# The first attention's convolutions by pairs with its weight work spread out, and unread matmuls in four stage tails and ahead of the third attention

## The reference

```
q, k, v = x @ Wq.T, x @ Wk.T, x @ Wv.T
q = silu(causal_group_conv(q, Wq_conv) + bq)   # 4 taps, one group of 128 channels per head
k = silu(causal_group_conv(k, Wk_conv) + bk)
gate, beta = sigmoid(x @ Wg.T + bg), sigmoid(x @ Wb.T + bb)
St = beta_t * St + k_t v_t^T                   # per head, over the 256 tokens of a sequence
out_t = (q_t . St) * gate_t
out = out @ Wo.T
```

## Time and profile before

| | us |
|---|---|
| three timed runs | 3417.91, 3407.55, 3426.61 |
| their median | 3417.91 |
| profiled execution, its own time | 3410.35 |
| its span, first to last instruction | 3408.5 |
| busy: TensorE, VectorE, GpSimd, ScalarE | 2928.4, 2177.0, 1583.2, 1431.4 |
| mean granted TensorE clock | 0.924 |

### The profile page before, as it was taken

One profiled execution on the slowest core, in us unless ns is written; L12 is line 12 of the kernel. 1 busy time (PEld: TensorE's weight loads), 2 busy tenths in 40 slices (PEclk: granted clock), 3 DMA queues, 4 the chain that ended last, 5 costly groups with the idle time before them and its releaser, 6 DMA issues. The chain is left out here.

```text
span 3408.5 us, 59487 instructions
## 1 busy us (share of the span) xinstructions
PE 2928.4 (86%) x20634; PEld 2564.9 (75%) x20634; DVE 2177.0 (64%) x5538; ACT 1431.4 (42%) x3043; POOL 1583.2 (46%) x1530
## 2 busy tenths in 40 slices
PE   8979999999999899795698977649997858976798
PEld 6859989998898788694487866647775746966687
DVE  6756666666666667665735656548886655665755
ACT  3344555555455433343523333335554334433342
POOL 2333444434444414634605435548887456450743
PEclk9989999999999999897798987959998878988899
DMA  2022212121211200332102333510002352330333
GB/s 70 1 72 55 61 53 68 52 62 52 62 55 49 74 27 1 97 121 63 36 2 80 94 108 90 145 44 2 2 2 69 88 141 81 113 109 3 93 99 97
DMA packets 129129, 220.88 MB, mean 65 GB/s; under 512 B 18609, under 2 KB 68145, under 8 KB 128881
## 3 DMA queue, kind: packets, MB, share of 16 engines
q1 hardware_dynamic: 95026, 147.47, 14.5%
q0 software_dynamic: 21216, 57.96, 6.6%
q10 hardware_dynamic: 12672, 12.58, 1.1%
HBM read 170.23 MB, written 47.72 MB: 64 GB/s over the span
## 5 line engine op out<-in xcount | busy, mean ns | idle before, releaser
L1632 POOL DMA_INDIRECT MXG<-dxn,IDX x250 | 237.3, 949 | 231.6 <-PE bank L1204 167.6
L1642 POOL DMA_INDIRECT YG<-dyo,POSI x192 | 187.4, 976 | 210.6 <-DMA dyo<-YS 111.9
L2491 POOL TENSOR_SCALAR SX<-SX,MN 128x256 f32<-128x256 f32 x256 | 233.7, 928 | 56.4 <-DVE MN L2415 56.3
L1615 POOL TENSOR_TENSOR MWL<-RAW,MWH 128x608 fp32r<-128x608 f32 (+2 forms) x118 | 181.6, 1547 | 42.5 <-ACT MWH L1307 36.2
L1971 POOL TENSOR_TENSOR QL<-QG,QH 128x512 fp32r<-128x512 f32 x64 | 82.9, 1296 | 248.7 <-ACT QH L1826 248.7
L2415 DVE CUSTOM_DVE_ANT_0 SX<-bank,FMASK 128x128 f32<-128x128 f32 (+1 forms) x512 | 156.1, 351 | 50.7 <-PE bank L2305 50.5
L515 PE MATMUL bank<-MWH,GH 128*128 x500 | 172.3, 345 | 8.3 <-issue 4.5
L1026 POOL TENSOR_TENSOR HL<-HID,HH 128x512 fp32r<-128x512 f32 x56 | 72.4, 1293 | 224.2 <-ACT HH L993 223.7
L515 PE MATMUL bank<-MWH,SHH 128*128 128x256 f32 x352 | 111.5, 317 | 73.6 <-POOL SHL L1486 25.4
L1940 POOL TENSOR_TENSOR HWL<-RAW,HWH 128x640 fp32r<-128x640 f32 x68 | 113.3, 1676 | 120.3 <-DVE DEC L1857 120.0
L1329 ACT ACTIVATE GH<-bank 128x256 fp32r<-128x256 f32 x250 | 96.7, 387 | 171.7 <-PE bank L1204 166.0
(11 more groups left out here) (451 smaller groups left out, 11263.0 us busy)
## 6 DMA issues: line engine op xcount, KB each, us to landing
dyo<-YS SPq DMA_DIRECT2D x250, 128.0 KB
RAW<-in_wheads SPq DMA_DIRECT2D x68, 320.0 KB
RAW<-in_eL SPq DMA_DIRECT2D x64, 304.0 KB
BB<-dgates SPq DMA_DIRECT2D x68, 256.0 KB, 3.6
GB<-dgates SPq DMA_DIRECT2D x68, 256.0 KB, 4.3
dxn<-XN ACTq DMA_DIRECT2D x16, 512.0 KB
RAW<-in_eL SPq DMA_DIRECT2D x32, 256.0 KB
RAW<-in_sL SPq DMA_DIRECT2D x18, 384.0 KB
```

What stands on the lines that cost most here:

```text
L1615: nc.gpsimd.tensor_tensor(MWL[:, at_:at_ + cols], RAW[:, n % RAW_SLOTS, 0:cols], f32(MWH[:, at_:at_ + cols]), ALU.subtract).then_inc(w_rea ...
L1632: nc.gpsimd.indirect_dma_start(MXG[:, n % XGS, :], None, dxn, bass.IndirectOffsetOnAxis(ap=IDX[:, b:b + 1], axis=0)).then_inc(x_in[n % XGS ...
L1642: nc.gpsimd.indirect_dma_start(YG[:, i % YGS, :], None, dyo[0:m.blocks * P, :], bass.IndirectOffsetOnAxis(ap=POSI[:, c * NT + t:c * NT + t ...
L2491: nc.gpsimd.tensor_scalar(part, part, MN[:, n % RING2, 1:2], None, ALU.subtract).then_inc(s_less1, 1)
```

## The change

In the first attention:

- q gets the pair form of k; `EH`, `EL`, `EV`, `DF` exist once for q and once for k. Keys come first everywhere (`KEYS_FIRST`).
- TensorE's order in step s is now: projections of k, q; result of s-2; values of s; scores of s-1; convolutions of k, q.
- VectorE's order is: differences of k, q; add(s-2); low parts of the values; weigh(s-1); scans; low part of scores; `post` of k, q; QG.
- GpSimd no longer waits for `dec_done`; it makes `tap_sums` of both, each in the step of its weight piece (n = 0 and n = 1).
- SP's rows for n = 3 move behind the next head's weight loads.

In the tails of four sparse layers, ten unread matmuls after each tile's `x_done`, for slots k > `m.late`: 8 of 16 tiles after L1, 14 after L2. Ahead of attn2, 20 unread matmuls, and 6 in each of six slots.

```diff
-PAIR_COL = HEAD_COLS
-ALL_COLS = HEAD_COLS + 2 * P
+PAIR_COLS = (HEAD_COLS, HEAD_COLS + 2 * P)
+ALL_COLS = HEAD_COLS + 4 * P
+KEYS_FIRST = (1, 0)
...
+                for t in range(NT if nx and k > m.late else 0):
+                    if k == m.slot_of(t):
+                        pe.wait_ge(b_kept, st.blocks + m.blocks)
+                        pe.wait_ge(x_done, st.xd + t + 1)
+                        warm(10, 5 if nx.kind == 'moe' else 2)
...
-                    for q in range(2):
-                        if q and (s or not first):
-                            pe.wait_ge(post_done, done + s)
+                    for j, q in enumerate(KEYS_FIRST):
+                        if s or not first:
+                            pe.wait_ge(both_kept, done * 2 + (2 * s - 1 + j))
                         for k in range(KC):
                             last = mm3(bank[q][:, :], weights(hh, PRE_COLS[q][k]), xt(k, n * W, W), k == 0, k == KC - 1)
                         last.then_inc(pre_done, 1)
-                    if s or not first:
-                        scores(s - 1, done)
+                    if s >= 2 or not first:
+                        result(s - 2, done)
...
-                    pe.wait_ge(pre_ready, done * 2 + (2 * s + 1))
-                    for c in range(CK):
-                        last = mm3(bank[2][:, :].rearrange('p (b t) -> p b t', b=2), weights(hh, CONV_COLS[0] + c * P),
-                                   (QPH[:, :, c:c + S], QPL[:, :, c:c + S]), c == 0, c == CK - 1)
-                    last.then_inc(conv_done, 1)
...
+                    if s or not first:
+                        scores(s - 1, done)
...
+                    for j, q in enumerate(KEYS_FIRST):
+                        pe.wait_ge(pre_ready, done * 2 + (2 * s + j + 1))
                         for c in range(2):
...
+                            last = mm3(bank[q][:, 0:S].rearrange('p (b j) -> p b j', b=2), weights(hh, PAIR_COLS[q] + (1 - c) * P),
+                                       moved(q, EVEN, c), c == 0, c == 1)
+                        last.then_inc(conv_done, 1)
+                        pe.wait_ge(d_lo, done * 2 + (2 * s + j + 1))
+                        if s or not first:
+                            pe.wait_ge(post_done, done * 2 + (2 * s - 1 + j))
+                        for part in EDGE:
+                            for c in range(2):
+                                last = mm3(bank[2 + q][:, part * S:(part + 1) * S].rearrange('p (b j) -> p b j', b=2),
+                                           weights(hh, CONV_COLS[q] + EDGE_TAPS[part][c] * P), moved(q, part, c), c == 0, c == 1)
+                        last.then_inc(conv_done, 1)
...
+                    differences(s, 0, done)
+                    differences(s, 1, done)
+                    if s >= 2 or not first:
+                        add(s - 2, done)
+                    values_lo(s, 0, done)
+                    values_lo(s, 1, done).then_inc(v_ready, 1)
                     if s or not first:
                         weigh(s - 1, done)
+                        dve.wait_ge(p_done, done + s)
                     dve.wait_ge(rows_in[n], at(nc.vector, i, 64, 32 * (hh + 1) + 16))
+                    decay(n, 0)
+                    decay(n, 1).then_inc(dec_done, 1)
                     if s or not first:
                         scores_lo(s - 1, done)
...
+                    post(s, 0, done)
+                    post(s, 1, done)
+                    dve.wait_ge(silu_done, done * 2 + (2 * s + 2))
                     nc.vector.tensor_tensor(QG[:, :], QS[:, :], GB[:, n * W:(n + 1) * W], ALU.mult).then_inc(qg_done, 1)
...
-                    if PIECES_AT[n]:
-                        pool.wait_ge(dec_done, done + (s + 1))
-                    if n == 0:
-                        pool.wait_ge(raw_in[1], i * 32 + 16 * (rounds + hh + 2))
-                        tap_sums(1 - hh, i * 4 + 2 * (hh + 1))
...
                     for q in PIECES_AT[n]:
+                        if q < 2:
+                            pool.wait_ge(raw_in[q], i * 32 + 16 * (rounds + hh + 2))
+                            tap_sums(1 - hh, q, i * 8 + (4 * (hh + 1) + 2 * q))
                         piece_lo(1 - hh, q, done + (st.pieces + PIECES * (hh + 1) + q + 1))
...
-            pe.wait_ge(xt_lo, (st.tr + 1) * HALF)
             pe.wait_ge(w_ready, st.pieces + 4)
             pe.wait_ge(prepared, 14)
+            warm(20, 2)
+            pe.wait_ge(xt_lo, (st.tr + 1) * HALF)
             for s in SLOTS2:
+                if s < 0:
+                    warm(6, 2)
```

More of the change, by code:

```diff
@@ L308, in build @@
         GB = r.put('GB', [P, T])
[L309 to L313, removed]
+        EH = [r.put(n, [P, 3, 2, H2 + 1], F32R) for n in ('QEH', 'KEH')]
+        EL = [r.put(n, [P, 3, 2, H2 + 1], F32R) for n in ('QEL', 'KEL')]
+        EV = [r.put(n, [P, 2, H2]) for n in ('QEV', 'KEV')]
+        DF = [r.put(n, [P, 2, 2, H2]) for n in ('QDF', 'KDF')]
         QG = r.put('QG', [P, W])
@@ L1747, in pair @@
[L1747 to L1753, removed]
-                        for c in range(2):
-                            last = mm3(bank[3][:, part * S:(part + 1) * S].rearrange('p (b j) -> p b j', b=2),
-                                       weights(hh, CONV_COLS[1] + EDGE_TAPS[part][c] * P), moved(part, c), c == 0, c == 1)
@@ L1757, in pair, with moved @@
-                    last.then_inc(conv_done, 1)
-                    if s or not first:
-                        result(s - 1, done)
+                    if s or not first:
+                        scores(s - 1, done)
+                    def moved(q, part, c):
+                        return EH[q][:, part, :, 1 - c:1 - c + H2], EL[q][:, part, :, 1 - c:1 - c + H2]
+                    for j, q in enumerate(KEYS_FIRST):
+                        pe.wait_ge(pre_ready, done * 2 + (2 * s + j + 1))
+                        for c in range(2):
+                            last = mm3(bank[q][:, 0:S].rearrange('p (b j) -> p b j', b=2), weights(hh, PAIR_COLS[q] + (1 - c) * P),
[9 more added lines that the diff above has]
+                        last.then_inc(conv_done, 1)
@@ L1763, in attn0_tensor @@
                 pair(i)
+            result(HK * NW - 2, 0)
             scores(HK * NW - 1, 0)
@@ L1809, in pair @@
                                              ACT.Copy).then_inc(w_hi, 1)
-                    if s or not first:
-                        scores_hi(s - 1, done)
                     act.wait_ge(v_done, done + (s + 1))
@@ L1835, in attn0_prepare @@
         def attn0_prepare(dve, st):
-            for hi in (QPH, QPL):
-                nc.vector.memset(hi[:, :, 0:CK - 1].bitcast(F32), 0.0).then_inc(prepared, 1)
-            for hi in (KEH, KEL):
-                nc.vector.memset(hi[:, :, :, 0:1].bitcast(F32), 0.0).then_inc(prepared, 1)
+            for part in EH + EL:
+                nc.vector.memset(part[:, :, :, 0:1].bitcast(F32), 0.0).then_inc(prepared, 1)
             dve.wait_ge(ld_c, 160)
@@ L1915, in pair @@
-                    values_lo(s, 1, done).then_inc(v_ready, 1)
-                    post(s, done)
-                    if s or not first:
-                        add(s - 1, done)
             pair(0)
@@ L1922, in attn0_vector @@
                 pair(i)
+            add(HK * NW - 2, 0)
             weigh(HK * NW - 1, 0)
@@ L1927, in attn0_pool, with tap_sums @@
         def attn0_pool(pool, st):
-            def tap_sums(parity, pairs):
-                taps = RAW[:, 1, 0:CK * P].rearrange('p (j two c) -> p j two c', two=2, c=P)
-                both = RAW[:, 1:RAW_SLOTS:2, PIECE:PIECE + P]
-                hi, lo = (a[:, parity, PAIR_COL:PAIR_COL + 2 * P].rearrange('p (j c) -> p j c', c=P) for a in (HWH, HWL))
+            def tap_sums(parity, q, pairs):
+                taps = RAW[:, q, 0:CK * P].rearrange('p (j two c) -> p j two c', two=2, c=P)
+                both = RAW[:, q:RAW_SLOTS:2, PIECE:PIECE + P]
+                cols = slice(PAIR_COLS[q], PAIR_COLS[q] + 2 * P)
+                hi, lo = (a[:, parity, cols].rearrange('p (j c) -> p j c', c=P) for a in (HWH, HWL))
                 nc.gpsimd.tensor_tensor(both, taps[:, :, 0, :], taps[:, :, 1, :], ALU.add).then_inc(pair_split, 1)
```

125 lines of the change are left out of this document (68 added, 57 removed).

## The result

The changed kernel takes 3481.86 us (median of four, 3472.78 to 3484.12), the kernel before, timed beside it, 3416.56 (3407.55 to 3426.61): ratio 1.0184, 95% interval 1.0164 to 1.0205. It is slower by 65 us; I forecast 3368, 48 us faster, and gave "slower" 0.05. The profiled spans are 3408.5 before and 3478.1 after.

The account below looks back on a forecast made before the run. TensorE was taken to set the first attention's pace. From 3415.6 us, attention -49.6 (-42.9 - 24.3 + 17.6) and unread matmuls +2 gave 3368 us; the forecast's own range was 3350 to 3385, the wider one 3335 to 3402.

Parts of the forecast that it names:

- The pair form: First attention, TensorE: query convolution as 18 products of 256 columns saves 0.67 us a step, 42.9 us in all.
- the 889 I had written: First attention: QG's first and last starts would be 63 x 14.1 = 889 us apart, not 938.
- The old wait for KL: First attention: TensorE's new order removes the scores' wait for GpSimd's low part of keys, 0.38 us a step, 24.3 us.
- The ring: First attention: scores of s-1 wait for add(s-2) over VectorE and ScalarE; 14.1 us, every second step waits, costing 17.6 us.
- the contention term: First attention: GpSimd's splits beside VectorE's two-SBUF-input operations cost VectorE about 0.1 us an operation, 0.2 us a step.
- my 14.1: First attention: predicted average step between QG starts, in us, against 14.89 before.
- Rival A: First attention: shared port blocks VectorE's scans behind a whole 1.56 us split; no attention gain, about 3418 us; chance 0.08.
- While gathers set the pace: Sparse tails: waiting for gathered rows covers two tiles' matmuls ahead of a group's transposes, except in each tail's third group.
- +3.5 us for four tails: Sparse tails: net price of their 440 unread matmuls, taken as +0.9 us a tail.
- The bound of +4.5 a tail: Sparse tails: upper limit per tail, two tiles' matmuls at the lower clock on the path; lower limit -2 us.
- Rival C: Tails and third attention: all 496 unread matmuls on the path as a serial chain, +112 us, 3478 us; chance 0.04.
- Ahead of the third attention: Before the third attention: 56 unread matmuls cost 4.5 us, a higher clock returns 6.0; net -1.5, bounds -3 and +5.9.

Follow-up runs that it names:

- scans in the wait: Changed kernel without unread matmuls, queries split first, VectorE's four scans moved into its wait before QG, GpSimd not waiting for them: 3371.39 us, ratio 0.9881 to the kernel before.
- the changed attention: Changed kernel without any of the 496 unread matmuls, its first attention as changed: ratio 1.0042 to the kernel before.
- queries first and the old wait: Changed kernel without unread matmuls, GpSimd splitting queries before keys and again waiting for the scans before weight pieces: ratio 0.9926 to the kernel before.
- the waits alone: Kernel before plus the tails' two TensorE waits (b_kept, x_done of each tile), without matmuls behind them: ratio 1.0035.
- five matmuls for each tile: Kernel before plus the tails' waits and five unread matmuls a tile (220), none ahead of the third attention: 3437.6 us, ratio 1.0072.
- the pairs in the old order: Kernel before with the query convolution by pairs, its order on each engine kept, no unread matmuls: ratio 1.01.

## Why the prediction was wrong

**The pair form** held. With the scans in the wait and the port free a plain step takes 13.58 us, and I had summed 13.55; the step on average fell from 14.89 to 14.13. So a gain of 48 us in the attention was there to be had; the changed kernel did not get it. That its 889.9 us for 63 intervals are the 889 I had written is luck. My number held 17.6 us for a ring that doesn't bind in this kernel. In their place stand the pauses at the loop's start, which I had put at nothing (at a head's start inside an iteration a step takes 14.91 us, at the jump from one iteration to the next about 16.85, where the kernel before took 15.57 at both; seven jumps, some 13 us), and part of the old wait for KL, which follows.

**The old wait for KL** was sized from one meeting, 0.38 us in the earlier trace rows, and put into all 64 steps. The view of waits of the kernel before has 45 waits from 240 to 1140, three steps in four; the step at a head's start has none. That is 48 x 0.38 = 18 us and not 24.3. Its idle time is 11.2 us in 900; the rest of the 0.38 is the first product after the wait starting up, and the plain step shows that it came back too (14.60 - 13.58 = 1.02, of which 0.67 is the pair form's).

**The ring** binds as I said: the add of s-2 releases the scores of s-1, and TensorE waits for it in 42 of some 60 steps; I had every second one.

**The failed step in the attention is the contention term**: "So GpSimd pays and VectorE gives about 0.1 an operation: 0.2 a step." It came from the earlier trace rows, QG of 0.79 us beside two splits. I read it as two operations sharing and took its length as the price. Read by time it says the contrary: the splits start at 675.51, the first would end at 677.07 (1.56 each), QG starts at 676.83 and ends at 677.62, 0.55 after that moment. In the changed kernel QG also ends 0.55 us after the split. And the earlier trace rows has the full block in its longest QG, 1.42 us: the one at 229.06, with a piece that had started 0.66 us earlier, again ended 0.55 after that piece. It was held up in the earlier trace rows too, only it came at the end of the first split and so lost 0.1, and got ahead of the second (3.56 for the two instead of 3.12). The price depends on when the two meet, and the change moved the meeting: keys first puts the split of the keys 0.57 us ahead of every QG, and without the wait for the scans a piece starts ahead of a scan. I had 0.2 us a step. Two kernels with the same order of VectorE, which differ in GpSimd's two splits alone, stand at 15.06 and 14.13: 0.93. In my own order of VectorE it is less: the changed attention's 15.15 fell to 14.57 with queries first and the old wait, 0.58. The 0.47 from there to my 14.1 is some 0.2 for the pauses, QG held up by late pieces in 47 of 64 steps, and a ring that still makes TensorE wait 31 times (20.8 us in 900); these weren't parted. The Trainium skill, SBUF — State Buffer, section "SBUF: two separate sides", has the port pair as an exclusive lock for the whole instruction; the traces agree (1.27 against 0.69 us, 1.73 against 0.40). Rival A was this mechanism, at 0.08. I had placed it on the scans only, and had no row for the order of the two splits. Its price, no gain in the attention, was some 15 us too kind.

**The failed step in the tails**: "While gathers set the pace this is covered by the wait for the next rows; for the third group of each tail the gathers are over, and it is on the path." The gathers don't set the pace after the first group: in the kernel before, the next one at 1573.67 had waited 5.54 us for the combine. The ring combine, matmuls, transposes, split, norm, combine does, so the 20 matmuls of each later group are on the path. I had +3.5 us for four tails; with the 56 of the third attention it is 47 in the changed kernel's trace. The bound of +4.5 a tail was for one group and so was no bound. Rival C names the mechanism, a serial chain, at 0.04. It asked for 67 us before the kernel becomes slower, because it still counted the attention's -50. That its time, 3478, lies 4 us from the measured one is luck: its terms were +112 and -50, and the traces have +47 and +16.

The runs divide the price as follows: the waits alone 7 us of the tails' table, five matmuls for each tile 19 more, ten (with the third attention's) 23 more again. Without the tie to x_done ten cost 10 us in all. So most of the price is the number of matmuls, paid because of their place between norm and transposes. Why the same lines cost 31 us on one kind of chip and 47 on the other wasn't found.

**Ahead of the third attention** I had -1.5, bounds -3 and +5.9; alone it is +3 by the ratio 1.0009, within what can't be told from nothing. The clock rose to 0.67 and not to 1, so the first scores came after 18.9 us and not after 14.

The sum, from 3416 us: attention +16 instead of -50, unread matmuls +47 instead of +2, and 3 us are left.

## What to carry to other kernels

Before an instruction of GpSimd is moved, list which VectorE instructions with two SBUF inputs run at its new time, and read an old meeting by its end times and not by its length: a short delay can be the tail of a full block. Work for the clock's sake must not be released by the event that also releases the real work behind it on the same queue; each wait put ahead of an instruction makes a ring of its own, and its turn has to be added up for every group, not for the last one. Before an order is blamed, swap one pair of instructions: here that alone was worth 0.93 us of a 15 us step. And when a loop's body grows, compare the loads of program code in the two traces: here it went from none an iteration to about 9.

## What the runs showed of the hardware

VectorE with two SBUF inputs stands still while a GpSimd split that started earlier is running, and ends 0.55 us (QG, 512 columns) after the split's end, wherever it started: QG took 1.42, 1.27 and 0.79 us with splits that had started 0.66, 0.57 and 1.34 us earlier, and in the pairs in the old order 1.17 with 0.94. In the other order GpSimd's second split waited: 3.56 us for two instead of 3.12. Subtractions of an SBUF tile from PSUM kept their time beside GpSimd: in the changed kernel VL took 1.29 us for two beside a split (660.64 to 661.83) and a tap sum, and the earlier trace rows has 1.28.

```profile
661.45 1.29 DVE L1860 TENSOR_TENSOR VL<-bank,VH 128x512 fp32r<-128x512 f32 x2 [0.28 <-ACT VH L1811]
```

The loop of the kernel before ran five iterations without a load of program code. With 48 more products in it 44 to 46 packets of 16 KB were loaded in five, and TensorE paused at the first product of each.

The same kernel took 3414 to 3418 us on some chips and 3351 to 3353 on others, with the difference spread over the stages behind the first attention (the four stretches of the table, without unread matmuls, have 337 and 315 to 317 us), while a step of the first attention was the same.
